# A transformer layer with routed experts: 32-byte records scattered and rows gathered by the experts, the first batch's row scores four heads at a time, and unread products in the drain

## The reference

```python
def attn(x):                       # 16 heads of 16
    scores = Q @ K.T / 4 + lam * (tanh(Q) @ J) @ tanh(K).T
    probs = softmax(where(causal, -inf, scores))
    return (probs @ V) @ Wo.T + bo
def ffn(x):                        # xf: 8192 tokens of 256
    logits = (layernorm(xf) * ln_scale + ln_bias) @ gate_w.T
    p1, p2, e1, e2 = top_2_of_8(softmax(logits))
    w = (p1, p2) / (p1 + p2 + 1e-5)
    out = swiglu(xf, sWg, sWu, sWd)                 # shared expert, inner width 512
    for r in (1, 2):
        out += w[r] * swiglu(xf, Wg[e_r], Wu[e_r], Wd[e_r])
x = x + attn(layernorm(x))
x = x + ffn(layernorm(x))
```

## Time and profile before

| | us |
|---|---|
| median of 3 runs | 2176.34 (2170.82 to 2176.91) |
| profiled execution | 2184.37 |
| its span in the trace | 2182.7 |
| PE busy | 1983.4 (91%) |
| DVE busy | 1246.0 (57%) |
| ACT busy | 1080.8 (50%) |
| POOL busy | 799.5 (37%) |
| stages in the trace: constants to 19.3, attention to 1190, front to 1515.8, experts to the end | |

### The profile page before, as it was taken

How to read it: one execution, slowest core, us unless ns; L and a number is a source line. 1 busy time by engine, 2 the same in 40 slices (tenths; PEclk the granted TensorE clock), 3 DMA queues, 4 the chain that set the end, 5 groups by cost and what they waited for, 6 DMA issues and landing times. The chain is left out here.

```text
span 2182.7 us, 48214 instructions
## 1 busy us (share of the span) xinstructions
PE 1983.4 (91%) x14698; PEld 1300.2 (60%) x14767; DVE 1246.0 (57%) x3875; ACT 1080.8 (50%) x2352; POOL 799.5 (37%) x1164
## 2 busy tenths in 40 slices
PE   2789999999999999999986999997999999999997
PEld 1344444554444444444444887875777777777776
DVE  5556677666677666676653964442454544545454
ACT  1155555555555555555542454451555555555553
POOL 3023333333233333233332046661444444444443
PEclk8589999999999999999987999998999999999999
DMA  7124443434433444434313345553873333333332
GB/s 238 42 84 117 133 127 113 127 112 120 138 114 120 115 118 138 126 115 129 107 62 105 116 160 206 196 177 101 216 201 55 58 53 57 56 54 59 53 55 35
DMA packets 156640, 246.08 MB, mean 113 GB/s; under 512 B 29408, under 2 KB 90592, under 8 KB 156480
## 3 DMA queue, kind: packets, MB, share of 16 engines
q1 hardware_dynamic: 120960, 189.24, 28.2%
q0 software_dynamic: 32064, 53.44, 11.9%
q10 hardware_dynamic: 3456, 1.34, 0.2%
HBM read 111.89 MB, written 90.50 MB: 93 GB/s over the span
## 5 line engine op out<-in xcount | busy, mean ns | idle before, releaser
L646 DVE CUSTOM_DVE_ANT_0 ps_rows<-ps_rows,maskrow 128x512 f32<-128x512 f32 (+3 forms) x1024 | 484.1, 514 | 309.6 <-PE ps_rows L501 308.8
L589 ACT ACTIVATE probs<-ps_cols 128x512 f32<-128x512 f32 (+3 forms) x1024 | 392.1, 435 | 394.1 <-PE ps_cols L512 387.5
L501 PE MATMUL ps_rows<-ks,qs 32*128 32x512 f32 (+3 forms) x2048 | 429.7, 494 | 85.3 <-DVE mx L646 47.4
L508 PE MATMUL ps_cols<-qs,ks 32*128 32x512 f32 (+3 forms) x2048 | 421.9, 488 | 2.5 <-ACT probs L589 2.4
L1590 POOL DMA_INDIRECT out_dram<-y_e,to x135 | 215.5, 1596 | 348.9 <-DMA out_dram<-y_e,to 227.6
L765 POOL TENSOR_TENSOR pace<-eps 1x1 f32<-1x1 f32 x256 | 57.9, 226 | 766.4 <-ACT probs L589 766.4
L501 PEld LDWEIGHTS ps_rows<-ks,qs 32*128 32x128 f32 x2048 | 162.2, 188 | 295.7 <-DVE mx L646 246.7
L512 PE MATMUL ps_cols<-mT,ones_r 32*128 32x512 f32 (+3 forms) x1024 | 287.3, 554 | 0.0
L1719 DVE TENSOR_TENSOR h_lo<-ps_h,h_hi 128x512 fp32r<-128x512 f32 x135 | 93.4, 692 | 231.5 <-ACT h_hi L1694 231.5
L1688 ACT ACTIVATE sg_e<-ps_ge 128x512 f32<-128x512 f32 x135 | 80.7, 598 | 261.2 <-PE ps_ge L1612 255.5
L525 PE MATMUL ps_o<-probs,vt 128*32 128x512 f32 (+3 forms) x2048 | 193.7, 450 | 0.8 <-POOL probs L767 0.8
(11 more groups left out here) (211 smaller groups left out, 3799.9 us busy)
## 6 DMA issues: line engine op xcount, KB each, us to landing
xs_d<-zrows SPq DMA_DIRECT2D x45, 408.0 KB, 2.9
xr<-xs_d POOLq DMA_DIRECT2D x135, 136.0 KB, 3.2
whi_d<-w_sh SPq DMA_DIRECT2D x16, 768.0 KB, 3.8
w_hi<-whi_d SPq DMA_DIRECT2D x24, 512.0 KB
xn<-in_L_attn_x_dram SPq DMA_DIRECT2D x16, 512.0 KB, 5.3
ks<-k_lin SPq DMA_DIRECT2D x64, 128.0 KB, 2.9
ks<-k_tan SPq DMA_DIRECT2D x64, 128.0 KB, 3.7
qs<-q_lin SPq DMA_DIRECT2D x64, 128.0 KB, 2.4
```

Source lines behind the costliest of these rows:

```text
L501: mm = nc.tensor.matmul(ps_rows[bank_of(row_no(g, it, h))][:, 0:(it + 1) * P], qs[at:at + STRIP, d.par, g, it * P:(it + 1) * P], ks[at:at ...
L508: nc.tensor.matmul(ps_cols[bank_of(col_no(n, s, e))][:, jt * P:S], ks[at:at + STRIP, b.par, gc, jt * P:(jt + 1) * P], qs[at:at + STRIP, b. ...
L589: nc.scalar.activation(probs[:, n % 2, 2 * (1 - s) + e, jt * P:S], ps_cols[bank_of(col_no(n, s, e))][:, jt * P:S], ACT.Exp).then_inc(exp_d ...
L646: nc.vector.tensor_tensor_reduce(out=bank, in0=bank, in1=maskrow[:, (TT - 1 - it) * P:S], scale=1.0, scalar=LOWEST, op0=ALU.add, op1=ALU.m ...
```

## The change

Three parts, made together.

**Records and gathers.** `xs_d` (135 x 128 rows of 1088 bytes) goes. In its place stands `meta_d` with 32-byte records of 8 floats: token's destination, share, its row in `x1_d`, and scale and shift of its layer norm. DVE writes scale and shift into `place` by two copies and works the place out in five small operations in place of one, twice. POOL scatters the 128 groups of 128 records one after the other as soon as `pos` and `place` are there, with no wait between them, reads all records back into `meta` by one transfer, makes integers of two columns and gathers the rows of slots 0 and 1 out of `x1_d`. ACT's two activations per tile, SP's `xw` loads, and 40 of the 45 zero transfers go (5 small ones remain). In the expert stage POOL gathers the rows of slot s+3 by an indirect transfer where it had a plain one, DVE normalises them (`xh`, 128 x 256) two slots ahead and copies source and destination numbers; share is read from `meta`, and PE transposes `xh`.

**First rows.** In the prologue one half issues four heads, into six banks (`ps_rows` and `ps_cols`, which nothing else uses there), and the second half returns at once.

**Unread products.** In the drain PE runs 42 products of 512 columns after the last product with V, and 3 more in each of steps 10 to 14. Nothing reads them.

With them the splits of Wk, Wq and Wv move from the attention stage into the constants block, between `bq_q` and `gws`, and `wq`, `wk`, `wv` are freed with it.

```diff
+            for at, (parts, whole) in enumerate(((wkp, wk), (wqp, wq), (wvp, wv))):
+                nc.gpsimd.tensor_copy(parts[:, 0], whole[:]).then_inc(s_parts, 1)
+                pool.wait_ge(s_parts, at * 2 + 1)
+                nc.gpsimd.tensor_tensor(parts[:, 1], whole[:], parts[:, 0].bitcast(F32), ALU.subtract).then_inc(s_parts, 1)
             for k in range(KT):
                 nc.gpsimd.tensor_scalar(gws[:, k], gw[:, k], sc[:, k:k + 1], None, ALU.mult)
...
+    def first_rows(d, u):
+        return d.off == 0 and u < STEPS * HG // 2
+
+    def row_bank(d, u):
+        return (*ps_rows, *ps_cols)[u % 6] if first_rows(d, u) else ps_rows[bank_of(u)]
...
+            if has_rows and first_rows(d, row_no(g, it, 0)):
+                if s == 1:
+                    return
...
+                if row_no(g, it, 3) >= 6:
+                    pe.wait_ge(max_done, row_no(g, it, 3) - 5)
+                for h in range(HG):
+                    at = STRIP * h
+                    mm = nc.tensor.matmul(row_bank(d, row_no(g, it, h))[:, 0:(it + 1) * P], ...)
+                    if h % 2:
+                        mm.then_inc(rows_ready, 1)
+                return
...
+        def fill(bank, n):
+            for _ in range(n):
+                nc.tensor.matmul(bank[:], ones_r[:], wkp[:, 0].rearrange("p k n -> p (k n)"), start=True, stop=True)
...
+                if b.off == TAIL and n == 0:
+                    pe.wait_ge(max_done, NB * STEPS * HG)
+                    fill(ps_rows[0], 42)
+                if b.off == TAIL and 10 <= n < 15:
+                    fill(ps_rows[0], 3)
...
-                if n in (9, 10, 11) and b.at_least(0) and b.at_most(NB - 2):
...
+                if b.off == 0 and 9 <= n < 9 + ZR:
+                    sp.dma_start(meta_z[n - 9], zrows[:]).then_inc(xs_zeroed, 16)
...
         pool.wait_ge(pos_ready, 2)
+        pool.wait_ge(placed, 2)
         for t in range(NT):
-            pool.wait_ge(normed, (t + 1) * 2)
             for r in range(2):
-                nc.gpsimd.indirect_dma_start(xs_d[:, :], ...)
+                nc.gpsimd.indirect_dma_start(meta_d[:, :], bass.IndirectOffsetOnAxis(ap=pos[:, t, r:r + 1], axis=0),
+                                             place[:, t, r], None).then_inc(scattered, 16)
+        pool.wait_ge(scattered, NT * 2 * 16)
+        pool.dma_start(meta[:].rearrange("p s w -> p (s w)"), meta_d.rearrange("(p s) w -> p (s w)", p=P)).then_inc(meta_in, 16)
+        pool.wait_ge(meta_in, 16)
+        nc.gpsimd.tensor_scalar(meta_i[:, :, 0], meta[:, :, TO], float(BEYOND), None, ALU.add).then_inc(meta_ready, 1)
+        nc.gpsimd.tensor_copy(meta_i[:, :, 1], meta[:, :, FROM]).then_inc(meta_ready, 1)
+        pool.wait_ge(meta_ready, 2)
+        for r in range(2):
+            nc.gpsimd.indirect_dma_start(xr[:, r], None, x1_d.rearrange("b p t d -> (b p t) d"),
+                                         bass.IndirectOffsetOnAxis(ap=meta_i[:, r, 1:2], axis=0)).then_inc(x_loaded[r], 16)
...
+        nc.vector.tensor_copy(place[:, :, :, SCALE], rstd2[:].unsqueeze(2).to_broadcast([P, NT, 2])).then_inc(placed, 1)
+        nc.vector.tensor_copy(place[:, :, :, SHIFT], nmr[:].unsqueeze(2).to_broadcast([P, NT, 2])).then_inc(placed, 1)
...
+        def gather(s):
+            if exists(s):
+                pool.wait_ge(xn_ready, s.v - 1)
+                pool.wait_ge(frm_ready, s.v - 1)
+                nc.gpsimd.indirect_dma_start(xr[:, s.par], None, x1_v, bass.IndirectOffsetOnAxis(ap=frm[:, s.quad], axis=0))\
+                    .then_inc(x_loaded[s.par], 16)
         def step(s):
-                pool.dma_start(xr[:, s.par], rows_of(xs_v, s.plus(2))).then_inc(x_loaded[s.par], 16)
+            gather(s.plus(3))
...
+            norm(s.plus(2))
+            source(s.plus(4))
+            destination(s.plus(-1))
```

More of the change, by code:

```diff
@@ L45 @@
 NSLOT = 2 * NT + NE - 1
-ZR = 3
+ZR = 5
 EARLY = 4
@@ L54 @@
 BEYOND = 1 << 14
-XW = D + 16
+MW = 8
+TO, SHARE, FROM, SCALE, SHIFT = range(5)
 class Batch:
@@ L150, in build @@
         slot_e = sbt(top, "slot_e", [1, NSLOT], I32)
+        meta = sbt(top, "meta", [P, NSLOT, MW])
+        meta_i = sbt(top, "meta_i", [P, NSLOT, 2], I32)
+        xr = sbt(top, "xr", [P, 2, D])
         xs_zeroed = top.enter_context(nc.semaphore("xs_zeroed"))
+        x_loaded = [top.enter_context(nc.semaphore(f"xe_loaded{r}")) for r in range(2)]
         with ExitStack() as mid:
@@ L795, in batch @@
                         .then_inc(xres_ready, 1)
-        for at, (parts, whole) in enumerate(((wkp, wk), (wqp, wq), (wvp, wv))):
-            nc.gpsimd.tensor_copy(parts[:, 0], whole[:]).then_inc(w_parts, 1)
-            pool.wait_ge(w_parts, at * 2 + 1)
-            nc.gpsimd.tensor_tensor(parts[:, 1], whole[:], parts[:, 0].bitcast(F32), ALU.subtract).then_inc(w_parts, 1)
         pool.wait_ge(shared_in, 3 * 16)
@@ L1180, in vector_unit, with front_stage @@
             self.norm(dve, s.plus(2))
-def front_stage(nc, ctx, sbt, shared, x1_d, out, xs_d, ident, ones, mv2, eps, rstd2, nmr, place, lgT, gws, gwb, pos, slot_e):
-    FIRST, RING, AHEAD, RANK_AT, ROWS_AT = NB, 8, 4, 2, 4
-    A_ROUND = (2, 1, 2, 1)
+def front_stage(nc, ctx, sbt, shared, x1_d, out, meta_d, meta, meta_i, xr, x_loaded, ident, ones, mv2, eps, rstd2, nmr, place, lgT, gws, gwb, pos, slot_e):
+    FIRST, RANK_AT = NB, 2
     def sb(name, shape, dt=F32):
@@ L1192, in sem @@
         return nc.alloc_semaphore(name)
-    row = [sb(f"row{q}", [P, 2, XW]) for q in range(RING)]
-    xw = sb("xw", [P, AHEAD, TT, D])
+    slot_i = sb("slot_i", [P, NT], I32)
+    slot_f = sb("slot_f", [P, NT])
     rr = sb("rr", [P, NT])
@@ L1217, in front_stage @@
     logits = sb("logits", [P, NT, NE])
-    cleared = sem("cleared")
-    xw_loaded = [sem(f"xw_loaded{r}") for r in range(AHEAD)]
-    normed = sem("normed")
-    scattered = [sem(f"scattered{q}") for q in range(RING)]
+    scattered = sem("scattered")
+    placed = sem("placed")
+    meta_in = sem("meta_in")
+    meta_ready = sem("meta_ready")
     filled = sem("filled")
@@ L1242, in front_stage @@
     ps_r, ps_n = (bank[:].rearrange("p (t e) -> p t e", e=NE) for bank in se.ps_t)
-    def tiles_of(s, i):
-        n = sum(A_ROUND)
-        first = (s.off - ROWS_AT) * n + sum(A_ROUND[:i])
-        many = A_ROUND[i] if s.off < FIRST - 1 else 2
-        return range(max(first, 0), min(first + many, NT)) if s.off >= ROWS_AT else range(0)
     @block.sync
     def _(sp):
-        def load_rows(bt):
-            if bt >= AHEAD:
-                sp.wait_ge(normed, (bt - AHEAD + 1) * TT * 2)
-            sp.dma_start(xw[:, bt % AHEAD], x1_d[bt]).then_inc(xw_loaded[bt % AHEAD], 16)
         se.load_in(sp, Batch(0, 0))
@@ L1263, in _ @@
         se.load_in(sp, Batch(0, 2))
-        for bt in range(AHEAD):
-            load_rows(bt)
-        loaded = AHEAD
         for s in range(FIRST + 1):
@@ L1269, in _ @@
                 se.load_in(sp, Batch(0, s + 2))
-            while loaded < NB and (loaded - AHEAD + 1) * TT <= (s - ROWS_AT) * sum(A_ROUND):
-                load_rows(loaded)
-                loaded += 1
             se.store(sp, Batch(0, s - 1))
@@ L1275, in _ @@
                 se.load(sp, Batch(0, s + 1))
-        for bt in range(loaded, NB):
-            load_rows(bt)
         for r in range(2):
@@ L1337, in _ @@
         nc.gpsimd.memset(lower[:], 1.0).then_inc(filled, 1)
-        for q in range(RING):
-            nc.gpsimd.memset(row[q][:, :, D:XW], 0.0).then_inc(cleared, 1)
-        pool.wait_ge(filled, 1)
+        nc.gpsimd.memset(place[:], 0.0).then_inc(filled, 1)
+        pool.wait_ge(filled, 2)
         nc.gpsimd.affine_select(out=lower[:], in_=lower[:], compare_op=ALU.is_gt, fill=0.0, base=0,
@@ L1519, in expert_stage @@
     to_ready = sem("to_ready")
-    share_ready = sem("share_ready")
-    x_loaded = [sem(f"xe_loaded{r}") for r in range(2)]
+    frm_ready = sem("frm_ready")
+    xn_ready = sem("xe_ready")
     tx_ready = sem("tx_ready")
@@ L1553, in exists, with column @@
         return s.at_least(0) and s.at_most(NSLOT - 1)
-    def rows_of(view, s):
-        return view[s.off] if s.fixed else view[bass.ds(s.v, 1)].rearrange("o p d -> (o p) d")
+    def column(t, s, c):
+        return t[:, s.off, c:c + 1] if s.fixed else t[:, bass.ds(s.v, 1), c]
     @block.sync
@@ L1592, in step @@
                     .then_inc(y_stored[d.par], 16)
+        gather(Batch(0, 2))
         over_slots(pool, step)
```

138 lines of the change are left out of this document (63 added, 75 removed).

## The result

The changed kernel takes 2302.83 us (median of 4 runs, 2298.72 to 2304.08) against 2176.62 us: a ratio of 1.0582 [1.056, 1.0605]. It is slower by 126 us where 36 us less were forecast. The profile shown here is of the run of 2304.08 us, whose span is 2302.2 us; the other three took 2298.72 to 2303.12 us.

A forecast was written before the change was run, and what follows sets the result against it. PE bounds the experts, neither PE nor DVE the prologue; PE idles in the drain, and all engines stall beside POOL's scatters. +3.0 - 11.8 - 3.5 - 25 + 1 = -36.3 us from 2176.3 gives 2140 us, range 2126 to 2172.

The forecast's parts named there:

- Records in place of rows: Front: without row traffic and 512 KB loads the stall beside POOL's scatters goes nearly whole, -25 of 27.4 us (-27 to -15).
- a choked front: Front: 161.6 us of unbroken scatters stall all engines, 129 us lost in place of 27, giving 2267 us; chance 0.11.
- The experts: Expert stage: the gather fits POOL's idle time and DVE has room for the normalisation, so 0 us (-1 to +2).
- The port rival: Expert stage: DVE's normalisation blocks POOL's scatter through the shared port, +31 us, 2171; within the 0.06 for POOL as bound.
- Routing: Front's routing: some ten small added DVE operations at 0.23 us each cost +1 us (0 to +2.3).
- Splits: Constants block: moved POOL splits end it 4.2 us later, a faster layer norm returns 1.2 us; net +3.0 us.
- First rows: Prologue: four heads at a time in six banks make DVE the bound, batch 0 starts earlier, -11.8 us (-14 to -8).
- the sum: Whole kernel: all terms together -36.3 us, with DVE's 24.58 us of work as the bound in the prologue.
- Drain: End of attention: unread products fill PE's idle 10.54 us and keep the full clock, net -3.5 us (-5; +1 if overshooting).
- about -1 together: Behind the drain: transpositions, gate products and the front's first products gain about 1 us from PE's full clock.

The follow-up runs named there:

- the runs of 16: The changed kernel with 16 POOL memsets of 128x512 after every 16 scatters: 2217.32 us, 328.9 us from first to last down product.
- the spacer: The changed kernel with a POOL memset of 128x512, into a tile nobody reads, behind each scatter: 2154.94 us, ratio 0.9911.
- the wait for landings: The changed kernel with POOL waiting before each scatter until the scatter two before it has landed: 2154.4 us, ratio 0.9912.
- the experiment: The kernel before with four heads at a time and the unread products alone, splits left in their old place, rows scattered as before: 2157.24 us, ratio 0.9928.
- The first experiment: The kernel before with four heads at a time, the unread products and the moved splits, rows scattered as before: 2160.43 us, ratio 0.9939.
- the spacer of 384 columns: The changed kernel with an unread POOL memset of 128x384 behind each scatter: 2146.81 us, ratio 0.9834 to the kernel before.

## Why the prediction was wrong, point by point

**Records in place of rows: this step failed.** It let the stalls of the earlier trace rows hang on the rows' traffic, for which it had no row, took the run of scatters as covered by other work, and expected 25 of the 27.4 us back; the span lost 124.4 us there instead. The bytes turned out not to matter (413.0 against 414.4 us), and the unbroken run was not covered by other work: it slowed that work. The named rival, a choked front, had the mechanism and came near in size: 129 us lost in place of 27, where two rounds of the changed kernel alone (between the down products of 1262.24, 1342.69 and 1449.68) took 80.4 and 107.0 us, 152 us more than two rounds of 17.54. It was given 0.11 because of one row: the 16 us of the earlier trace rows with 11 us of scatters and no loss. That row can't carry this. From POOL's timeline of the kernel before, the start and the end of the train of scatters that it shows:

```profile
1382.51 1.30 POOL L1355 DMA_INDIRECT xs_d<-row,pos  x1 [4.11 <-ACT row L1323]
...
1388.72 0.96 POOL L1355 DMA_INDIRECT xs_d<-row,pos  x1 [0.30 <-ACT row L1323]
...
1397.58 0.96 POOL L1355 DMA_INDIRECT xs_d<-row,pos  x1 [0.30 <-issue]
```

It is a train of 12 in 16.0 us behind a pause of 4.11 us, with only its last 8, in 9.8 us, at 1.27 us. Seven other trains of 12 in the same trace, in 15.2 to 15.6 us, left PE idle for 1.0 to 2.9 us each, all of it ended by "issue"; one more, of 16.0 us, did not. So a train there is about as long as the choke needs to build up, and one without loss is a near miss. The changed kernel, too, loses nothing in its first 20 us, and the runs of 16 nothing in their first 8. A short run proves nothing about one of 161 us. The rows that spoke for the choke, all three engines slow at once and well again when a run of scatters ended, stood in the prediction and were outweighed by that one. The loss that it asked for to make the kernel no faster, 38.7 us, was passed almost four times over.

What stays open is the inside of it: whether the pace or the number under way fills something up (the spacer and the wait for landings both help), and by what path an indirect issue on POOL holds up the others. The profile names the waits "issue" and "remote", and has no row behind them; the loads of instructions in the trace do not explain them.

**The experts: right that POOL doesn't bind, wrong by some microseconds.** 667.4 us against 660.6, so +6.8, and -1.9 on the way there, where 0 (-1 to +2) was forecast. A slot takes 4.81 us in place of 4.79; over 134 slots that is 3.6 us, whose cause no run settled. The start takes 3.8 us longer, from the first gate product to the first inner product of DVE (8.79 us against 5.03). The port rival fell. From the changed kernel's timeline, DVE's normalisations in two slots:

```profile
1908.30 0.41 DVE L1752 TENSOR_SCALAR xh<-xr,meta 128x256 f32<-128x256 f32 x1
...
1913.11 0.61 DVE L1752 TENSOR_SCALAR xh<-xr,meta 128x256 f32<-128x256 f32 x1
```

and POOL's beside them:

```profile
1907.89 1.59 POOL L1597 DMA_INDIRECT out_dram<-y_e,to  x1 [2.00 <-issue]
1909.78 0.99 POOL L1582 DMA_INDIRECT xr<-x_d,frm  x1 [0.30 <-issue]
...
1912.53 1.59 POOL L1597 DMA_INDIRECT out_dram<-y_e,to  x1 [1.76 <-DMA out_dram<-y_e,to]
```

The scatter takes 1.59 us beside the normalisation, as before. In nine slots the normalisation starts first and overlaps the scatter; the scatter then takes 1.59 to 1.71 us, with a median of 1.59. By the rule of the Trainium skill ("SBUF — State Buffer", section Who interferes with whom) such an operation can block the scatter for its whole length, 0.41 us; no such length shows here. The other way round something does: the normalisation takes 0.41 us where no scatter or gather is beside it, and up to 0.74 where one is. The gather lies in the idle time, as the step said, and two indirect issues in 4.8 us show no choke.

**Routing: small, as said.** +1 forecast for DVE's added operations; between the first two down products 21.26 us lie in place of 20.98.

**Splits: right.** +3.0 forecast, +3.7 in the trace, 3.4 to 4.0 in the traces of the experiment. From the changed kernel's timeline, `jb` of POOL and the layer norm of DVE, answering to the earlier trace rows:

```profile
22.58 0.93 POOL L296 TENSOR_SCALAR jb<-jb,lam_b 128x256 f32<-128x256 f32 x1
28.97 1.38 DVE L670 TENSOR_SCALAR xn<-xn,mv,rstd 128x256 f32<-128x256 f32 x4 [9.71 <-DMA xn<-in_L_attn_x_dram]
```

`jb` starts 4.2 us later, as worked out, and the layer norm is back at 1.38 us.

**First rows: right.** -11.8 forecast, -12.4 measured, and batch 0 at 91.44 where "near 91" was forecast. Busy time in the changed kernel, of the stretch that answers to the first line of the earlier trace rows, and of its last part before batch 0:

```profile
58.00:101.00 43.00, 27.33 (x147) 13.30 (x146) 28.86 (x115) 9.25 (x15) 0.78 (x2) 0.72 0.20 58
68.00:91.40 23.40, 10.09 (x68) 5.09 (x64) 20.67 (x92) 2.22 (x3) 0.00 (x0) 0.62 0.00 1
```

The first line holds some 10 us of batch 0. In the second DVE is busy 20.67 of 23.40 us and PE 10.09: DVE is now the bound, as the sum took it.

**Drain: right in its own products, wrong at the front's start.** -3.5 was forecast in all; it is -3.5 to the front's first product and -1.4 with the front's start. PE's timeline of the changed kernel, answering to the earlier trace rows:

```profile
1156.80 0.43 PE L557 MATMUL ps_o<-probs,vt 128*32 128x128 f32 x8 [0.82 <-POOL probs L804]
1157.16 9.81 PE L546 MATMUL ps_rows<-wkp,ones_r 128*128 128x512 f32 x42
...
1167.68 1.97 PE L472 MATMUL ps_m<-wo,onT 128*128 128x256 f32 x8 [0.71 <-DVE onT L734]
1170.43 1.99 PE L472 MATMUL ps_m<-wo,onT 128*128 128x256 f32 x8
```

Busy time behind them, columns as above:

```profile
1167.00:1183.00 16.00, 12.38 (x81) 9.58 (x82) 6.82 (x25) 3.19 (x5) 3.54 (x7) 1.00 0.18 66
1183.00:1190.00 7.00, 5.59 (x18) 4.38 (x17) 4.36 (x13) 3.08 (x4) 0.00 (x0) 0.51 0.81 273
```

Behind 42 unread products in 9.81 us the granted clock is 1.00 to 1183 us, where it was 0.50 from 1176 to 1184 in the kernel before, and "out" takes 1.97 us in place of 3.75. But the front's start gave 2.1 us back: PE now reaches the front before DVE, its first transposition waits 1.98 us there, the granted clock is 0.51 from 1183 to 1190, and the first six gate products take 2.93 us where they took 1.65. The step claimed a gain there (part of "about -1 together") and got a loss; that the -3.5 comes out without it is luck. The first experiment has most of it (+1.5 us), with the rows still scattered.

With the spacer of 384 columns, which takes the choke and the old stall away, the kernel comes near what was forecast: 2146.81 against 2179.39 us on the same chip is -32.6 us, where the sum was -36.3. The stall's 25 us so were there to be had, but by pauses and not by fewer bytes.

## What to carry to other kernels

When all engines slow together and their idle time ends by "issue" or "remote", look for a long run of indirect issues on POOL, and space them (here 1.62 us apart), break them into short runs (here 4 and a pause), or keep two under way, before anything is done about bytes or rows. A wait that breaks up such a run is a brake that the kernel may live by: before taking it away, ask how long the run gets without it. And a stretch without loss is evidence only for runs as short as that stretch.

## What the hardware showed that was not expected

- Indirect issues by POOL at 1.27 us, one after the other, slow PE to one product in 2.8 us, ACT and DVE to one operation in 15 to 30 us. PE's first gap comes 11 to 22 us behind the first issue; at 1.50 us a milder choke begins some 30 us into the run, and at 1.62 us none came in 207 us. It does not depend on bytes (32 or 1088 a row), rows (16 or 128) or direction, and 128 plain transfers by POOL at 0.57 us show none.
- It outlasts the run: the last scatter of the changed kernel ends at 1417.8, and PE goes on in single steps until some 1433 (from 1433.7 it issues 13 products in 3.63 us).
- The same attention code (batch 0 to its last product) took 1061.8 us in the first experiment and 1065.4 us in the changed kernel, with 1065.1 in the kernel before. The granted clock between 101 and 200 us goes with it, 0.97 in the first experiment against 0.91 and 0.89; what sets it there stayed open.
